# Layer 3's main convolution in the three-product form that layers 1 and 2 use

## What is computed

```python
def _layer(x, style, w, b, mw, mb, typ):
    s = style @ mw.T + mb
    weight = SCALE * w * s[:, None, :, None]
    demod = lax.rsqrt(jnp.sum(weight * weight, axis=(2, 3)) + EPS)
    weight = weight * demod[:, :, None, None]
    ...   # typ 'same' | 'upsample' | 'same' | 'downsample', each with 3 taps, + b
def _L3_ffn_ref(x, U1, V1, U2, V2, b1, b2):
    P = jnp.einsum('bsh,hr->bsr', x, U1)
    H = jnp.einsum('bsr,rf->bsf', P, V1) + b1
    gate, up = (H[..., :INTER], H[..., INTER:])
    act = jax.nn.silu(gate) * up
    Z = jnp.einsum('bsi,ir->bsr', act, U2)
    return jnp.einsum('bsr,rh->bsh', Z, V2) + b2
x = x + _L0_ffn_ref(_L0_cond_ref(x, ...), ...)   # and so on, up to layer 3
x = x + _L3_ffn_ref(_L3_cond_ref(x, ...), ...)
```

## Time and profile before

| | us |
|---|---|
| median of 3 runs | 2101.85 |
| lowest, highest | 2090.32, 2104.71 |
| the profiled execution, its own time | 2104.27 |
| its span in the trace | 2102.1 |

### The profile page before, as it was taken

The page is one execution under the profiler, slowest core; times in us unless marked ns, Lnnn a source line. Parts: engine busy times, 40 slices in busy tenths (PEclk is TensorE's granted clock), DMA queues, the critical chain, the costliest instruction groups (busy, mean ns, idle before and its releaser), DMA issues. The chain is left out here.

```text
span 2102.1 us, 32166 instructions
## 1 busy us (share of the span) xinstructions
PE 1963.4 (93%) x10207; PEld 1663.8 (79%) x10207; DVE 1302.0 (62%) x2326; ACT 962.2 (46%) x1547; POOL 377.8 (18%) x457
## 2 busy tenths in 40 slices
PE   5799968799999989998899999988999999999999
PEld 4688834799999978886788888877888878878886
DVE  6887878777776763327677666656555444444443
ACT  4488744455555431104344444434666544433441
POOL 4122211211111100002111111112121223322331
PEclk9999989999999999999999999999999999999999
DMA  7567547321112155444211122123233211142114
GB/s 195 172 196 193 175 164 242 96 70 60 60 62 88 51 176 159 136 135 143 74 59 60 60 62 73 56 69 118 100 100 109 86 50 45 53 143 87 46 45 163
DMA packets 118608, 222.30 MB, mean 106 GB/s; under 512 B 18336, under 2 KB 65184, under 8 KB 117792
## 3 DMA queue, kind: packets, MB, share of 16 engines
q1 hardware_dynamic: 102048, 212.36, 32.0%
q10 hardware_dynamic: 16512, 9.31, 1.6%
HBM read 159.04 MB, written 62.59 MB: 105 GB/s over the span
## 5 line engine op out<-in xcount | busy, mean ns | idle before, releaser
L2665 DVE SCALAR_TENSOR_TENSOR f_prod<-ps,b,f_gate 128x512 f32<-128x512 f32 (+1 forms) x88 | 66.1, 751 | 160.3 <-ACT f_gate L2605 160.3
L2706 POOL TENSOR_TENSOR x_lo<-f_prod,x_hi 128x512 fp32r<-128x512 f32 (+1 forms) x88 | 113.8, 1293 | 278.3 <-ACT x_hi L2612 278.3
L125 POOL TENSOR_TENSOR rows<-l_EY,ones 128x4 f32<-128x4 f32 x128 | 31.0, 242 | 730.0 <-ACT rows L1349 368.5
L2535 PE MATMUL ps<-pt_hi,v_hi 128*128 128x512 f32 (+1 forms) x352 | 137.5, 391 | 1.7 <-PEq L638 1.7
L2535 PE MATMUL ps<-pt_lo,v_hi 128*128 128x512 f32 (+1 forms) x352 | 137.3, 390 | 0.0
L2535 PE MATMUL ps<-pt_hi,v_lo 128*128 128x512 f32 (+1 forms) x352 | 137.2, 390 | 0.0
L2605 ACT ACTIVATE f_gate<-ps,b 128x512 f32<-128x512 f32 (+1 forms) x88 | 60.7, 690 | 156.0 <-PE ps L2535 156.0
L1570 DVE SCALAR_TENSOR_TENSOR rows<-ps,dem3e,l_middle 128x512 f32<-128x512 f32 x60 | 45.1, 752 | 121.4 <-ACT l_middle L1318 97.8
L125 POOL TENSOR_TENSOR XE<-rows,ones 128x8 f32 (+1 forms) x96 | 21.1, 243 | 533.6 <-DVE rows L1780 259.7
L1088 PE MATMUL ps<-l_u_hi,l_g_hi 128*128 128x512 f32 x272 | 111.5, 410 | 5.4 <-DVE l_g_lo L1604 5.2
L1088 PE MATMUL ps<-l_u_hi,l_g_lo 128*128 128x512 f32 x272 | 108.5, 399 | 0.0
(11 more groups left out here) (407 smaller groups left out, 5844.6 us busy)
## 6 DMA issues: line engine op xcount, KB each, us to landing
x<-rows SPq DMA_DIRECT2D x64, 512.0 KB, 2.9
xin<-x SPq DMA_DIRECT2D x96, 256.0 KB, 4.0
rows<-x SPq DMA_DIRECT2D x48, 512.0 KB, 4.1
out<-rows SPq DMA_DIRECT2D x32, 512.0 KB, 2.6
v<-in_ffn_v SPq DMA_DIRECT2D x84, 128.0 KB, 2.6
xin<-in_x SPq DMA_DIRECT2D x16, 512.0 KB, 6.1
xb<-in_x SPq DMA_DIRECT2D x16, 512.0 KB, 3.3
x<-xb SPq DMA_DIRECT2D x16, 512.0 KB, 2.6
```

The source lines that it names most:

```text
L2535: mm = nc.tensor.matmul(ps[0:m, 2 * g + gu, :], v1sp[ws][:, s, r, gu, 0:m], pt[ms][:, r, cols], start=(k == 0), stop=(k == 5))
L2665: v.scalar_tensor_tensor(prod[0:m, g, :], ps[0:m, 2 * g + 1, :], b1[0:m, 1, bass.ds(2 * i + g, 1)], gate[0:m, g, :], ALU.add, ALU.mult).th ...
L2706: nc.gpsimd.tensor_tensor(asp[1][0:m, g, :], prod[0:m, g, :], asp[0][0:m, g, :].bitcast(F32), ALU.subtract).then_inc(al_ready, 1)
```

## The change

```diff
-FAST = (1, 2)
+FAST = (1, 2, 3)
```

## The result

| | before | after |
|---|---|---|
| median, us | 2101.93 | 2205.34 |
| lowest, highest | 2090.32, 2104.71 (4 runs) | 2202.63, 2209.06 (4 runs) |
| span of the profiled execution | 2102.1 | 2201.7 |

What follows compares the result with a forecast made beforehand. TensorE bounds layer 3's conv phase; the change makes VectorE's chain the bound. 50.0 (pairs) + 5.4 (first step) - 1.3 (last pair) + 22.5 (clock) = 76.6 us slower, forecast 2179 us, range 2148 to 2198.

Steps and rivals of the forecast that it cites:

- What bounds the kernel: Layer 3's conv phase: TensorE bounds it before, other engines' chain hidden by 1.0 us; afterwards VectorE's chain sets the pair.
- 18.80: Layer 3, one pair from main to main after the change: 18.80 us against 15.23, +50.0 us over 14 steps.
- TensorE's saving of 1.30 a pair: Layer 3's main convolution: about 0.65 us saved per half, 1.30 a pair, 19.5 us over 15 pairs.
- the rival of the gain as drawn: Layer 3's chain stays hidden and TensorE gives back 19.5 us: 2082 us, chance 0.03.
- so I take 11.89 whole: VectorE from L1570 of half 1 to L1564's end in layer 3: 11.89 us, taken unchanged from a layer 1 pair.
- costed at nothing: Layer 3 work priced zero: pt_lo, next pair's x_lo, input loads, SP's second staging tile, clears of the even tiles.
- The clock, 15 x 1.5: Layer 3: idle TensorE before main lowers its clock every pair, 1.5 us each over 15 idle times, +22.5 us.
- the waits of 1438.00 and 1453.14: TensorE idle times of 3.67 and 1.95 us in the trace before, each followed by a granted clock of 0.50.
- 6.85 in my sum: Layer 3, path from main's start to the join of half 1, set by ScalarE: 6.85 us.
- The price taken from the FFN of pair 0: Layer 3, pair 0's 24 FFN products took 4.48 us instead of 2.97, giving 1.5 us per clock fall.
- First step and last pair: Layer 3: step from pair 0 to 1 costs +5.4 us; the last pair keeps only the gain, -1.3 us.
- The sum: Whole kernel: 50.0 + 5.4 - 1.3 + 22.5 = 76.6 us slower, forecast 2179 us, chance 0.55.

Runs made afterwards that it cites:

- experiment 3: Changed kernel with layer 3's GpSimd bias addition behind VectorE's last split and 13 filler products in TensorE's wait: 2154.05 us, ratio 1.0279.
- experiment 10: Changed kernel, bias addition late, 11 filler products, VectorE splitting even inputs (own semaphore) and differences ahead of `a` and z, half 0's shared product last: 2141.49 us.
- experiment 4: Kernel before, with layer 3's main in pairs 1 to 15 cut to 18 products of 256 columns a half, nothing else new: 2085.31 us, ratio 0.9937.
- experiment 1: Changed kernel where layer 3's GpSimd bias addition (L1951) waits until VectorE has finished the last split (L1564): 2176.94 us, ratio 1.0368.
- experiments 1, 6 and 7: The 6: kernel before, with GpSimd's bias addition of layers 1 and 2 waiting for VectorE's split of h: 2119.64 us, ratio 1.0088.
- Experiment 2: Changed kernel with 18 unused products of 512 columns filling TensorE's wait behind layer 3's `ffn`, addition left in place: 2176.16 us, ratio 1.036.
- experiment 7: Kernel before, with GpSimd's bias addition behind the filter splits in layer 1 and behind the gates in layer 2: 2093.95 us, ratio 0.9974.
- experiment 8: Kernel before, with GpSimd's bias addition waiting for the gates in layer 2 only: 2094.82 us, ratio 0.9983.

## Why the prediction was right, and where it failed

- **What bounds the kernel.** Right. The change moved the bound of layer 3 from TensorE to VectorE's chain; main waits for L1564, as said, TensorE idles 4.9 us in front of it and is busy 74% of the phase (4 to 5 us and 70 to 75% were named). Experiments 3 and 10 show it by size: 18.87 for 18.80, and one microsecond of chain is one of the pair.
- **TensorE's saving of 1.30 a pair.** Too large for the old order, where experiment 4 measured 0.79, since the low part of `a` comes late. In the changed kernel that split stands ahead of main and the chain sets the end, so this error didn't enter the time; it made the rival of the gain as drawn about 5 us too good (14.6 measured for 19.5).
- **The chain, "so I take 11.89 whole".** This is the step that failed. The instructions and their order were right, but GpSimd's addition was in none of my lists: L1951 was not among what is costed at nothing, nor looked at beside the new instructions. It added 1.38 a pair (13.27 for 11.89). The trace of before already had the hold-up: sums of up to 2.98 us in layer 2. And it had what makes layer 3 differ from the copy. In layer 1 the addition (L1990) waits for a load; in layer 3 it starts right behind GpSimd's edge columns, in the kernel before too:

```profile
1557.70 0.20 POOL L125 TENSOR_TENSOR rows<-l_EY,ones 128x4 f32<-128x4 f32 x1 [4.11 <-ACT rows L1349]
1557.85 2.40 POOL L1951 TENSOR_TENSOR rows<-rows,l_last_bias 128x1024 f32<-128x1024 f32 x1
```

There VectorE ran only splits with an operand in PSUM beside it (L1546, L1611). The new form puts the sums at that place, so the two meet in every pair and not now and then. The Trainium skill, "SBUF — State Buffer", section "Who interferes with whom", says that a VectorE instruction with two SBUF inputs contends with a GpSimd instruction that reads SBUF, that the port which they share is an exclusive lock, and that the order of issue decides which one is blocked. The row of the first sum agrees: begun behind the addition, it is done only after it; and in experiments 1, 6 and 7 it is always the instructions with both operands in SBUF that stretch.
- **The clock, 15 x 1.5.** Right in kind, too small. The fall came in every pair, as forecast from the waits of 1438.00 and 1453.14. From main's start to the join of half 1 the path took 8.3 and 9.3 us in turns, 8.8 on average, against 6.85 in my sum: 1.97 a pair, not 1.5. Half 0 alone lost 1.86 at half clock (4.01 for 2.15). The price taken from the FFN of pair 0 covered 2.97 us of products; here up to 3.69 us lie in the slow stretch. Experiment 2 gives 29 us for the whole effect.
- **The Trainium skill's section on the clock's swings** ("TensorE: Matmul & The Clock Gate", "HAM oscillation — how this bites in real kernels") says that each burst behind such a wait begins slow, again and again; the starts at 1572.21 and 1593.94 agree (0.66 and 0.50 behind them).
- **First step and last pair.** +5.26 for +5.4 (the terms written there add up to 5.3). The last pair took 0.2 longer, just its two terms: -1.3 from the products and the fifteenth 1.5 of the clock.
- **The sum.** By these measured terms: 1.38 + 0.47 = 1.85 us a pair more than forecast, times 14 is 26; this is, within a microsecond, the distance from the 76.6 of the forecast to the 102.3 of the bill. The range was too narrow because its upper end took in the clock alone, and no case in which the chain is longer than in layer 1.

Open is why short and long slow stretches come in turns; it was not tried.

## What to carry to other kernels

A form that saves matmul columns by more elementwise work must be paid from the slack of the elementwise chain, and that slack is the time from the last input to the last split, not 100% minus the busy share: here 1.0 us of slack met a path through VectorE that grew by 4.6 us even without the hold-up and the slow clock (1.0 of slack and the 3.6 by which experiment 3's pair is longer), while VectorE was 55% busy. When a stage is priced from a copy elsewhere in the same kernel, read several pairs of the copy and take the spread. Then look, in the stage that is changed, at what GpSimd does there and what starts it, and lay it beside each new VectorE instruction that reads two operands from SBUF. A wait of TensorE that is made new can cost twice, by itself and by the slow products behind it, as the 4.9 us did here each time, and the 1.6 us of experiment 3 did not; filling it with idle products gave back 29 us of 103, but not the wait.

## What the runs showed of the hardware that I had not expected

An addition of GpSimd (128x1024, 2.4 us) holds up a VectorE instruction with both operands in SBUF by nearly as much as it has left: the pair sums took 2.17 for 0.76 (1.41 more, with 1.55 left), the splits of the filter 2.80 for 1.42 (1.38, with 1.59 left), the split of z 1.18 for 0.74 (0.44, with 0.64 left), and where it began between two sums they took 2.97. The splits of x took 3.53 for 1.41. Beside the same addition L1593, L1555 and L1556, with one operand in PSUM, kept 1.22 and 0.68. GpSimd is slowed itself when it comes second: 2.72 for 2.39 in experiment 1. Where the addition waits for a load, whether the two meet differs from pair to pair and from execution to execution: two to six of the fifteen sums of layer 2 are long in the eight traces in which this layer is unchanged, with up to 3.5 us a pair, and these are the traces whose layer 2 takes 443 to 456 us. With the addition put where it can't meet the sums it takes 445 (experiment 7) and 443 (experiment 8). The runs of experiment 7 lay within 7 us of each other, those of the kernel before within 13; in experiment 8 they lay within 13 again, so that a smaller spread is not shown.
